# Windowed attention scores: products of 64 queries by 128 keys replaced by products of 32 queries by 96 keys

## What is computed

```python
bk2 = concatenate([previous window of k, own window of k])     # 128 keys for 64 queries
mask = (it < jb) | (it > jb + w) | (jb == -1)                  # it: query position, jb: key position, w = 64
sim = jnp.einsum('bhwie,bhwje->bhwij', bq, bk2) * QK_SCALE
sim = jnp.where(mask, -jnp.finfo(sim.dtype).max, sim)
attn = jax.nn.softmax(sim, -1)
out = jnp.einsum('bhwij,bhwje->bhwie', attn, bv2)
```

## Time and profile before

| | us |
|---|---|
| median of 3 runs | 4252.39 |
| lowest, highest | 4247.05, 4257.46 |
| the profiled execution | 4249.61 |
| its span, first to last instruction | 4247.7 |
| PE busy | 3943.0 (93%) |
| DVE busy | 2921.3 (69%) |
| ACT busy | 2606.4 (61%) |
| POOL busy | 1239.5 (29%) |
| mean granted clock | 0.976 |

### The profile page before, as it was taken

How to read it: one execution, slowest core, us unless ns; L and a number is a source line. 1 busy time by engine, 2 the same in 40 slices (tenths; PEclk the granted TensorE clock), 3 DMA queues, 4 the chain that set the end, 5 groups by cost and what they waited for, 6 DMA issues and landing times.

```text
span 4247.7 us, 86120 instructions
## 1 busy us (share of the span) xinstructions
PE 3943.0 (93%) x30808; PEld 2603.9 (61%) x30808; DVE 2921.3 (69%) x10261; ACT 2606.4 (61%) x6872; POOL 1239.5 (29%) x809
## 2 busy tenths in 40 slices
PE   8979489899987999999999999999999999999986
PEld 5659346566664666666666666666666666666664
DVE  3542356777776877777777777777777777777773
ACT  2213146666674766777667667676667667676662
POOL 1103300000004433334343334343343434343330
PEclk9979799999998999999999999999999999999998
DMA  5002210000002000111011100111010100111010
GB/s 187 23 23 74 61 58 2 6 16 17 16 2 63 21 21 24 44 39 28 16 52 28 39 21 20 49 39 28 16 52 26 41 21 19 49 40 28 16 36 18
DMA packets 94306, 146.62 MB, mean 35 GB/s; under 512 B 17908, under 2 KB 59744, under 8 KB 93504
## 3 DMA queue, kind: packets, MB, share of 16 engines
q1 hardware_dynamic: 90480, 131.80, 10.7%
q0 software_dynamic: 3408, 9.31, 0.9%
HBM read 79.36 MB, written 11.40 MB: 21 GB/s over the span
## 4 chain that ended last, share of the span: by engine, by line
PE 54%; DVE 8%; POOL 4%; issue 2%; DMA 1%; ACT 0%; SPq 0%; DVEq 0%; POOLq 0%
PE psum L496 18%; PE psum L591 9%; PE psum L476 7%; PE psum L575 6%; PE psum L608 5%; PE psum L554 4%; PE psum L529 4%; POOL f_rn L898 3%; DVE f_rot L716 2%; DVE f_rot L718 1%; DVE f_ss L723 1%; DVE f_xn L813 1%; DVE f_prob L759 1%; PE psum L597 1%; DVE f_prob L787 1%
## 5 line engine op out<-in xcount | busy, mean ns | idle before, releaser
L496 PE MATMUL psum<-f_wqkv,f_xsT 128*128 128x512 f32 x2304 | 1077.9, 596 | 4.3 <-ACT f_raw L641 2.7
L893 POOL TENSOR_TENSOR f_raw<-f_rot 128x512 f32<-128x512 f32 x384 | 488.3, 1272 | 1690.4 <-DVE f_rot L718 1690.4
L655 ACT ACTIVATE f_prob<-f_prob,f_nb,f_rq 128x128 f32<-128x128 f32 x1536 | 744.7, 492 | 37.9 <-DVE f_nb L772 37.0
L496 PEld LDWEIGHTS psum<-f_wqkv,f_xsT 128*128 128x128 f32 x2304 | 401.0, 191 | 323.9 <-issue 319.3
L898 POOL TENSOR_TENSOR f_rn<-f_ss,f_half_pow 128x32 f32<-128x32 f32 x96 | 522.9, 5446 | 11.1
L759 DVE CUSTOM_DVE_ANT_0 f_prob<-psum,f_band 128x128 f32<-128x128 f32 x1536 | 353.6, 286 | 130.0 <-PE psum L529 128.8
L591 PE MATMUL psum<-f_xnT,f_w 128*128 128x512 f32 x960 | 437.5, 595 | 2.2 <-ACT f_hT L678 1.1
L639 ACT ACTIVATE f_sq<-psum 128x512 f32<-128x512 f32 x384 | 228.3, 594 | 227.8 <-PE psum L496 227.5
L787 DVE TENSOR_SCALAR f_prob<-f_prob,f_rs 128x128 f32<-128x128 f32 x1536 | 342.6, 287 | 13.6
L575 PE MATMUL psum<-f_wo,f_oT 128*128 128x256 f32 x1536 | 347.4, 379 | 1.7 <-ACT f_v L641 0.9
L716 DVE TENSOR_TENSOR f_rot<-f_raw,f_tab 128x512 f32<-128x512 f32 x384 | 333.7, 869 | 15.4 <-DMA x_before_mlp<-x_all 15.4
(11 more groups left out here) (249 smaller groups left out, 7268.7 us busy)
## 6 DMA issues: line engine op xcount, KB each, us to landing
f_v_near<-f_v SPq DMA_DIRECT2D x168, 256.0 KB, 3.4
f_wqkv<-in_Wqkv SPq DMA_DIRECT2D x36, 512.0 KB, 5.9
w_moe_W<-in_L_ffn_W SPq DMA_DIRECT2D x2, 4096.0 KB, 21.9
f_w<-in_W SPq DMA_DIRECT2D x12, 640.0 KB
f_wo<-in_Wo SPq DMA_DIRECT2D x6, 1024.0 KB, 6.5
f_xs<-x_all SPq DMA_DIRECT2D x24, 254.0 KB
expert_rows<-m_y SPq DMA_DIRECT2D x39, 128.0 KB, 1.7
h_mask_int<-in_mask_BxSxS_ik SPq DMA_DIRECT2D x16, 256.0 KB, 2.6
```

The costliest lines, as they stand in the source:

```text
L496: mm = nc.tensor.matmul(ps.ap(step), xsT[:, c, t * P:(t + 1) * P], wqkv[:, c, i * HALF:(i + 1) * HALF], start=c == 0, stop=c == KC - 1)
L655: ex = nc.scalar.activation(pr, pr, ACT.Exp, bias=nb[:, t % 2, h:h + 1], scale=rq8[:, t, h:h + 1], accum_out=sums[:, t % 2, h:h + 1])
L893: nc.gpsimd.tensor_tensor(raw[:, (4 * t + i) % 8, :], rot[:, n % 2, 0, :], rot[:, n % 2, 1, :], ALU.add).then_inc(rope_done, 1)
```

## The change

The scores of a pair of slots are taken in four groups of 32 queries (`ask` 0 to 3) in place of two halves of 64. A product is 64 rows by 32 columns, with at most 96 keys streaming, and its position in the array is given explicitly. The new helper `near_columns` returns the column in PSUM at which the scores go, the first key and the key after the last. The keys are now in natural order (64 before, then 64 own for the first half), so `key_blocks` goes, `band` is loaded in two DMAs in place of three, and the two halves of `v_near` change places. In the first tile the groups 0 and 1 have 32 and 64 keys, since none lie before the sequence; `kT` is no longer cleared by DVE at the stage's start. The columns of PSUM that no product writes are masked by `band`.

```diff
--- before.py
+++ after.py
@@ -115,8 +115,7 @@
     def load_first(self, sp):
         sp.dma_start(self.rope[:], self.tabs["rope"]).then_inc(self.consts, 16)
         band, W = self.tabs["band"], P // 2
-        sp.dma_start(self.band[0:W, :, 0:W], band[0:W, :, P:P + W]).then_inc(self.consts, 16)
-        sp.dma_start(self.band[0:W, :, W:P], band[0:W, :, W:P]).then_inc(self.consts, 16)
+        sp.dma_start(self.band[0:W], band[0:W, :, W:P + W]).then_inc(self.consts, 16)
         sp.dma_start(self.band[W:P], band[W:P, :, P:2 * P]).then_inc(self.consts, 16)
         self.load_scales(sp, 0)
         for i in self.PARTS:
@@ -175,6 +174,7 @@
     HID = w["W2"].shape[1]
     H, DH = 16, 64
     WINDOW = W = 64
+    R = 32
     TB = 4
     NB = x_all.shape[1] // TB
     KC = D // P
@@ -368,14 +368,10 @@
         def tile(it, t):
             return it % NB * TB + t
 
-        def key_blocks(ap, t, half):
-
-            blocks = ap.rearrange("p (k j) -> p k j", j=W)
-            if half:
-                return blocks[:, 2 * t:2 * t + 2, :]
-            if t:
-                return blocks[:, 2 * t - 1:2 * t + 1, :][:, ::-1, :]
-            return blocks[:, 0:2 * TB:2 * TB - 1, :]
+        def near_columns(t, ask):
+
+            first = t * P + ask * R - W
+            return ask % 2 * R + max(-first, 0), max(first, 0), R * (ask + 1) + t * P
 
         out_tiles = out.rearrange("b (t p) d -> p (b t) d", p=P)
         block = ctx.enter_context(nc.Block())
@@ -390,9 +386,9 @@
             def copy_near(ps, it, off, t):
 
                 wait_drained(sp, ps, ("qkv", off, t, 5), it)
-                sp.dma_start(v_near[0:W, t, :], v[0:W, t, :]).then_inc(near_ready[t], 16)
+                sp.dma_start(v_near[W:P, t, :], v[0:W, t, :]).then_inc(near_ready[t], 16)
                 if t + 1 < TB:
-                    sp.dma_start(v_near[W:P, t + 1, :], v[W:P, t, :]).then_inc(near_ready[t + 1], 16)
+                    sp.dma_start(v_near[0:W, t + 1, :], v[W:P, t, :]).then_inc(near_ready[t + 1], 16)
 
             def shift(ps, it, b):
 
@@ -520,17 +516,19 @@
                             pe.wait_ge(ps.sem_drained(key), ps.before(key, it))
                         for m in (0, 1):
                             for n in range(2):
-                                for half in range(2):
+                                for ask in range(P // R):
+                                    col, first, last = near_columns(t, ask)
                                     for i in range(2):
                                         key = step + (i,)
                                         rows = slice(i * DH, (i + 1) * DH)
-                                        asks = slice(half * W, (half + 1) * W)
-                                        at = (2 * m + n) * P
-                                        mm = nc.tensor.matmul(ps.ap(key)[asks, at:at + P],
+                                        asks = slice(ask * R, (ask + 1) * R)
+                                        at = (2 * m + n) * P + col
+                                        mm = nc.tensor.matmul(ps.ap(key)[asks, at:at + last - first],
                                                               qT[rows, 2 * (g + m) + n, asks],
-                                                              key_blocks(kT[rows, 2 * (g + m) + n, :], t, half),
-                                                              start=True, stop=True)
-                                        if m == n == half == 1:
+                                                              kT[rows, 2 * (g + m) + n, first:last],
+                                                              start=True, stop=True,
+                                                              tile_position=(i * DH, ask * R))
+                                        if m == n == 1 and ask == P // R - 1:
                                             mm.then_inc(ps.sem_filled(key), 1)
                     elif kind == "pt":
                         m = step[2]
@@ -687,7 +685,6 @@
             def evac(out, in_):
                 return nc.vector.tensor_copy(out, in_)
 
-            nc.vector.memset(kT[:, :, (TB - 1) * P:TB * P], 0.0)
             nc.vector.memset(v_near[:, 0, :], 0.0)
             nc.vector.memset(xsT[:, 1, 0:1], 0.0)
             nc.vector.memset(xs[0:1, 0, :], 0.0)
@@ -696,7 +693,7 @@
             nc.vector.memset(half_pow[:], -0.5).then_inc(pads, 1)
             dve.sem_inc(ss_ready, NQ)
             dve.sem_inc(x_ready, NB)
-            dve.wait_ge(consts, 64)
+            dve.wait_ge(consts, 48)
             dve.wait_ge(saved, 16)
             for steps, ps, it, _ in phases:
                 for step in steps:
@@ -873,7 +870,7 @@
         @block.gpsimd
         def _(pool):
             pool.wait_ge(pads, 1)
-            pool.wait_ge(consts, 64)
+            pool.wait_ge(consts, 48)
 
             for steps, ps, it, _ in phases:
                 for step in steps:
```

## The result

| | before | changed |
|---|---|---|
| median, us | 4250.8 (4247.05 to 4257.46, 4 runs) | 4227.33 (4226.76 to 4227.52, 4 runs) |
| the profiled execution, us | 4249.61 | 4227.51 |
| its span, us | 4247.7 | 4225.6 |
| ratio to before | | 0.9942 (95% interval 0.993 to 0.9955) |

The changed kernel is 0.58% faster. The forecast was 4214, in a range of 4205 to 4256: the direction was right, and about 60% of the expected gain came.

A forecast was written before the change was run, and what follows sets the result against it. PE was taken to bound the kernel, except in a DVE and POOL stretch of each body. 4249.6 less 35.7 (214 ns times 167 pairs) and 1.0 (memset) gave 4212.9; with the median 2.8 higher it said 4214, range 4205 to 4256 us.

The forecast's parts named there:

- The sum: Whole kernel: profiled 4249.6 less 35.7 for the scores and 1.0 for the memset gives 4212.9 us.
- the likeliest case: Scores: all eight positions stream together; 4206 to 4225 us, likeliest 4214, chance 72%.
- seven of eight pairs count: Chain of a body: 7 of 8 score pairs lie on it, 167 of 192; the eighth lies in the DVE stretch.
- PE's wait for `xn`: Layer norm's transposes in each body: PE's wait for DVE's result grows from 1.7 to 1.9 us.
- 82 ns to a round: Scores: a round of eight products is paced by its 96 streamed columns and takes 82 ns.
- the first pitch: Start of a pair's scores: first round to second takes 108 ns, as the first weights are not hidden.
- A: Rival, slower: score records come no faster than the mean pace already seen; 4388 us, chance 6%.
- B: Rival, slower: at most four positions stream at once, 16 rounds of four in the scores; 4318 us, chance 10%.
- C: Rival, no change: a product's two streams are grouped in fours, a pair takes 1078 ns; 4244 us, chance 10%.
- D: Rival: the given position is read otherwise than the operands' rows say, showing as wide weights; chance 2%, within the slower cases.
- The two rules: Starts of products on PE: a floor of about 25 ns from start to start, against 4 ns for packed positions.
- six more of 82: Scores of a pair: six rounds after the first pitch at 82 ns each, 494 of the 890 ns.

The follow-up runs named there:

- f1: Changed kernel with the pair of slots 8 and 9 scored as before (64 queries by 128 keys): 4231.56 us, the changed kernel rerun beside it 4229.13.
- f2: Changed kernel with the pair of slots 10 and 11 scored as before: 4229.22 us, the changed kernel rerun beside it 4229.13.
- e1: Changed kernel with the score products of m = 1 left out, 16 products to a pair in place of 32: 4163.14 us.
- e2: Changed kernel with each score product streaming only its first 32 keys, still 32 products to a pair: 4194.42 us.
- e3: One part of the change alone: 32 queries, positions of 64 rows by 32 columns, but all 128 keys of the half; ratio 1.0009 to the kernel before.
- f3: Changed kernel with the first 4 products of each pair 64 queries by 128 keys, 24 narrow ones after: 4268.82 us, ratio 1.0042 to the kernel before.

## Why the prediction was right or wrong

**The sum against the trace.** The profiled executions differ by 22.1 us. From the first `xn` to the last (1477.5 to 4199.3 before, 1474.1 to 4177.0 now) it is 2721.8 against 2702.9, 18.9 less. That is 22 bodies with 0.86 each; one body that now took 0.8 longer than the rest is nearly made up for by one that took 0.3 longer before, and by 0.4 in the last, shorter stretch. 1.7 us come from ahead of the last stage, where nothing was changed; 1.1 from the memset, and 0.6 from the first body. The rest, 0.2 the other way, lies in the tail.

The sum itself is loose at its end: 4212.9 and 2.8 are 4215.7, not 4214, and the range of the likeliest case has the 2.8 in its 4225 but not in its 4206.

**What binds.** Right: seven of eight pairs count, and f1 and f2 show that just the pair in the stretch of DVE and POOL is free. DVE stayed behind PE and passed the gain on, as the earlier trace rows said. Wrong in a detail: PE's wait for `xn` was to grow from 1.7 to 1.9, and stayed at 1.67. What the eighth pair saves goes into the short wait for `f_prob` before it, from 0.04 to 0.12 us.

**Eight positions together.** Right, 82 ns to a round, starts 6.6 ns apart, the first pitch 106 ns for 108, the last record 242. Rivals A, B and C are out by these rounds, and D by the shape 64*32 of the records. The two rules that the prediction set against each other are settled for this case: 32 records start within 0.318 us in e1, 10 ns apart on average, less than half of the 25 that the Trainium skill gives as a floor (TensorE: Matmul & The Clock Gate, Part 1). Its Part 3 has 4 ns between starts of packed positions, which is nearer to the 6.6 within a round here.

**The step that failed.** The term "six more of 82", with the overlap of eight positions taken to last through all 32 products. Three rounds came 82 apart as it says (they start at 189, 272 and 354), and within the last of them the products from the 18th on came late. The pair took 996 ns and not 890, a gain of 108 ns in place of 214 (148 in the two pairs of a sequence's first tile, where the early products are shorter). Five pairs of 108 and two of 148 make 0.84 us to a body, against the 0.86 that the bodies show; times 24 that is 20 to 21 us, and with the memset 21 to 22, where the sum had 36.7. I had checked that the starts fit into a round, but not how many products the engine takes on ahead. The rows of before could not show it: a pair had 16 products, and each round of four took 109 ns. It would have needed the products under way to be counted: 8 rounds of 82 ns ask for a product every 20.6 ns, and with 349 + 35 ns from a product's start to its slot being used again, 17 slots give one every 22.6, and 16 one every 24.0.

**What the window is** was not settled. The 16.6 ns stood in the base, in e2, e3 and f3, for three different lengths of a product; in each the last products of the third set come at the first product's end, 35 ns, and steps of 16.6 ns from the 18th on, so they follow that end and not the time. Whether 16 or 17 products fit is open, since in e2 the 17th is late too. The Trainium skill (TensorE: Matmul & The Clock Gate, the table at its head) gives TensorE a queue of 64. A product is two loads and two streams, so 16 products would fill it; that is an estimate from that page. The late 17th of e2 fits it, and no run here shows what is counted.

**Rival chances.** The ends of the range held. The likeliest case's own lower bound on the gain, 4225, was missed by 2 us: it allowed rounds of 90 ns, and the late products amount to 97, (996 - 315)/7.

## What to carry to other kernels

Cutting products into smaller positions pays by the columns that are no longer streamed, and only as long as the engine's window covers them: count the products under way, divide the life of one by the number that fit (here some 384 ns by 17), and compare that with the time from product to product that the positions would allow (here 20.6 ns). Keep positions of one width together; a change of width cost 0.11 us here. And a semaphore on which the bounding engine stands names the last link, not the bound: moving PE's step behind more work won 0.4 us of 1.7, because the queue behind the releaser was the bound. Waits too short for the list of waits can be the ones that take up a gain: look at the starts.

## What the runs showed of the hardware

- Eight positions of 64 rows by 32 columns stream float32 together at full pace: 82 ns for 96 columns, 109 for 128 (e3), with starts 6.6 ns apart. With 32 columns the streams of one position followed 32 ns apart (e2).
- 16 or 17 products of two loads and two streams can be under way on PE; behind them one enters every 16.6 ns, from some 35 ns after the oldest has ended (the changed kernel, e2, e3, f3).
- Going from 64-column to 32-column positions held PE up for 0.11 us (f3); that the array drains there is inferred.
- Whole runs of one kernel differed by up to 13 us, while nearly all bodies of a run agreed to 0.02 us; profiled runs entered the last stage between 1288 and 1301 us. A small change in a late stage is better read from the period of its bodies.
